# Attention stage of a decoder: block probabilities without zeros, another order on TensorE, doubled parts of z

## The chip, the cores and the metric

The kernel runs on one core of one Trainium2 chip, in one launch. The metric is the device time of one execution in microseconds (us), from runs of the kernel before and the kernel after on the same chip. The engines are TensorE (PE in the profile, with its weight loads in a row of their own, PEld), VectorE (DVE), ScalarE (ACT), GpSimd (POOL) and SyncE (SP), whose queue issues the DMAs.

## What is computed

A two-layer decoder over 32 sequences of 64 tokens with width 256 (2048 tokens, 16 tiles of 128). The change lies in the first of its stages, the self-attention of layer 0: 16 heads of 128, causal, with a layer norm ahead of it.

```
x = x + attention(layernorm(x))                       # the first stage
q = einsum('bpd,hde->bphe', x, W_Q) + b_Q             # k and v alike, with W_K and W_V
scores = einsum('bqhe,bkhe->bhqk', q, k) / sqrt(128)  # 64 x 64 per sequence and head
attn = softmax(where(causal, scores, -100000))
z = einsum('bkhe,bhqk->bqhe', v, attn)
out = einsum('bqhe,hed->bqd', z, W_O) + b_O
```

The stages after it (a cross attention and a feed-forward network, then layer 1) are the same in both kernels.

## The kernel before

**Tiles and units.** A tile holds 128 tokens, that is two sequences of 64. `stage_L0_attention` works in 64 units: 16 heads times 4 groups of 4 tiles (512 tokens). A matmul that needs more precision than fp32r has runs in three products of high and low parts (`PARTS`): the tokens `xnT`, the weights `w_parts` and `wv_parts` and the weighted values `zT` each exist as a high and a low part. Scores, turned probabilities and weighted values are plain fp32 matmuls.

**One unit** goes through these steps:
- TensorE: `project` (queries and keys of 4 tiles, 6 matmuls of 512 columns each), and for the even heads also `values`, which serves two heads at once: 12 matmuls of 256 columns before the queries (tiles 0 and 1) and 12 after the keys (tiles 2 and 3). `scores`: 8 matmuls, one per sequence; the two sequences of a tile write to the two halves of the partitions. `turn`: 4 transposes of the probabilities. `weigh`: values times probabilities, one matmul per tile. `output`: 12 matmuls with W_O.
- ScalarE copies out of PSUM (`v_copy(0)`, `q_copy`, `k_copy`, `v_copy(1)`, `probT_copy`), takes the exponential (`exponent`) and makes the high part of z (`z_high_part`).
- VectorE masks the scores, finds the greatest and subtracts it (`shift`), sums, inverts and multiplies (`normalise`), makes the low part of z (`z_low_part`) and adds the output to the tokens (`add_out`).

**Zeros.** The probabilities of one tile lie in a 128x128 square `prob[:, t, :]` with two 64x64 blocks on its diagonal, one per sequence; the rest was set to zero once (line 674), so that one transpose and one matmul per tile serve both sequences.

**Order of the work.** Each engine has a list of parts with a lag, and `run_steps` goes through it: in step s, part p handles unit s - lag. Within a step an engine takes its parts in the order of the list, strictly one after the other; semaphores hold it where another engine is not ready. Before the change TensorE's list is project (lag 3), turn (4), scores (3), output (5), weigh (4). A round is 8 steps: units 0 to 3 belong to an even head (with values: a **value step**), units 4 to 7 to an odd one (without: a **plain step**).

**Beside it.** In the same lists runs the preparation of two things. First, the weights of a later head: SP loads them (`load`, lines 432 to 449), ScalarE makes the high part (`split_high`, lag 0, at the second unit of each head; for an even head also the value weights, line 615), GpSimd the low part (`split_low`). Second, the dequantisation of the last layer's weights (`Dequantiser`), one of 16 pieces per 4 units: VectorE works in phases 0 to 3 (lines 2466 to 2487) at lag 3, ScalarE in phases 0 (two instructions, lines 2496 and 2498) and 3 (line 2503) at lag 4, GpSimd adds (`gpsimd_sum`, behind `split_low` in its queue) and makes the low part; SP stores the piece.

The load of a head's weights first waits for the outputs of the head two before it, whose buffers it takes; it stands on SP's queue, and ScalarE's splitting waits for the same count and for the load:

```
wait(sp, o_full, (h - 2) * G + G)                      # line 434, SP, before the loads of head h
act.wait_ge(w_in[slot], (rnd + 1) * 48)                # line 610, ScalarE, unit 4 h + 1
wait(act, o_full, u - 5)                               # line 611
```

`prob`, `zT` and `z_ps` are single buffers; each of the eight PSUM banks has one use (`q_ps`, `k_ps`, `v_ps`, `s_ps`, `pT_ps`, `z_ps` and two of `o_ps`).

Of the kernel before, what the change touches and what calls it, by code (L numbers as in the profile page):

```python
# [16 lines left out]
P = 128  # L17
# [257 lines left out]
def split_tokens(core, parts, mv, factor, tag, column_step=1, beside=None, high_beside=None):  # L275
# [7 lines left out]
    with ExitStack() as ctx:  # L283
# [6 lines left out]
        def rows(t):  # L290
            return turned[:, t % 4, 0:D].rearrange("p (c q) -> p c q", c=NC)

        @block.vector
        def _(dve):
            def low(t):
                dve.wait_ge(high_done, t + 1)
                nc.vector.tensor_tensor(parts[:, 1, :, t, :], rows(t), parts[:, 0, :, t, :], ALU.subtract) \
                    .then_inc(low_done, 1)
# [17 lines left out]
        def _(act):  # L316
            for t in range(NT):
                act.wait_ge(turned_done, t + 1)
                nc.scalar.activation(parts[:, 0, :, t, :], rows(t), ACT.Copy).then_inc(high_done, 1)
# [85 lines left out]
def stage_L0_attention(core):  # L405
# [6 lines left out]
    with ExitStack() as octx:  # L412
        oroom = Room(nc, octx, "s1")
        xnT = oroom.sb("xnT", [P, 2, NC, NT, P], F32R)
# [65 lines left out]
        split_tokens(core, xnT, mv, rstd, "s1t", beside=low_weights, high_beside=high_weights)  # L480
        with ExitStack() as ctx:
# [3 lines left out]
            v = room.sb("v", [P, G, TG, 2, E])  # L485
# [5 lines left out]
            prob = room.sb("prob", [P, TG, P])  # L491
            probT = room.sb("probT", [P, TG * P])
            zT = room.sb("zT", [P, 2, TG * P], F32R)
# [3 lines left out]
            s_ps = room.ps("s_ps", [P, 512])  # L497
            pT_ps = room.ps("pT_ps", [P, 512])
            z_ps = room.ps("z_ps", [P, 512])
            o_ps = room.ps("o_ps", [P, 2, 512])  # L500
            (q_full, k_full, v_full, s_full, pT_full, z_full, q_out, k_out, v_out,
             masked, maxed, shifted, exped, summed, inverted, prob_done, pT_out, z_high, z_low, o_out, zeroed) = room.sems(
                "q_full", "k_full", "v_full", "s_full", "pT_full", "z_full",
                "q_out", "k_out", "v_out", "masked", "maxed", "shifted", "exped", "summed", "inverted",
                "prob_done", "pT_out", "z_high", "z_low", "o_out", "zeroed")
# [19 lines left out]
            def _(pe):  # L525
# [3 lines left out]
                def values(u, g, half):  # L529

                    wait(pe, v_out, u + g + half)
                    for n in range(2):
                        t = 2 * half + n
                        for c in range(NC):
                            for px, pw in PARTS:
                                last = nc.tensor.matmul(v_ps[:, n * 2 * E:(n + 1) * 2 * E],  # L536
                                                        xnT[:, px, c, g * TG + t, :], wv_parts[:, pw, c, :, :],
# [4 lines left out]
                def project(u, rnd, k):  # L542
# [7 lines left out]
                    for m, ps, full, out in ((0, q_ps, q_full, q_out), (1, k_ps, k_full, k_out)):  # L550
                        wait(pe, out, u)
                        for c in range(NC):
                            for pw, px in PARTS:
                                last = nc.tensor.matmul(ps[:, :], weights(slot, pw, m, c),  # L554
# [4 lines left out]
                    if slot == 0:  # L559
                        values(u, g, 1)  # L560
# [2101 lines left out]
```

## Time and profile before

| | us |
|---|---|
| three timed runs | 1759.6 to 1762.84, median 1762.19 |
| the profiled execution's own time | 1760.59 |
| its span, first to last instruction | 1758.8 |
| TensorE busy in the span | 1589.2 (90%) |
| VectorE busy | 1088.3 (62%) |
| ScalarE busy | 863.8 (49%) |
| GpSimd busy | 672.6 (38%) |

The profile has one row per instruction or group of instructions: the line of the kernel, the engine, the operation, what it writes and reads, how many (x), how long. PE rows are matmuls, PEld rows the loads of their stationary operand; the two overlap, and the ends of matmuls are modelled, so distances between starts tell more than durations. "128x64" tiles are parts of TensorE's array that work side by side (rows x columns; printed as 128*64). "Idle before" is how long the engine stood before the row, and what released it. "issue" is idle time in which the engine waited for nothing that the profile shows. The first stage's loop lies between about 30 and 562 us of the span.

### The profile page before, as it was taken

How to read it: one execution, taken by the hardware profiler on the slowest of the kernel's cores; microseconds unless marked ns; L12 is line 12 of the kernel's file. 1: busy time of each engine (PE TensorE's matmuls, PEld its weight loads, DVE VectorE, ACT ScalarE, POOL GpSimd, SP SyncE). 2: the span in 40 equal slices, each digit the busy share in tenths (PEclk: the TensorE clock that was granted, in tenths of full speed). 3: DMA queues.
4: the chain of work that ended last, by engine and by line, in shares of the span. 5: the costliest groups of instructions: out<-in, count | busy, mean ns of one | idle time of the engine just before them, and what ended most of it. 6: DMA issues, size and time to landing. Idle time of an engine off the chain costs nothing. (4 is left out here: it accounts for less than half of the span.)

```text
span 1758.8 us, 37012 instructions
## 1 busy us (share of the span) xinstructions
PE 1589.2 (90%) x14664; PEld 1283.0 (73%) x14664; DVE 1088.3 (62%) x1734; ACT 863.8 (49%) x1466; POOL 672.6 (38%) x527
## 2 busy tenths in 40 slices
PE   6999999999997887799999797899997898999998
PEld 4888888888885665687788564566664675888887
DVE  5767777677777888566442468999994564111111
ACT  3545555555453565555422346666672674222222
POOL 0121211211212662531432255999994430233332
PEclk9999999999998998899999799999998897999999
DMA  3011111011112300000102020000000900000000
GB/s 104 16 64 52 43 63 59 33 63 60 39 56 83 104 2 26 8 12 11 40 1 105 23 69 1 1 2 1 2 1 26 358 17 1 1 13 9 4 12 12
DMA packets 72351, 70.26 MB, mean 40 GB/s; under 512 B 24816, under 2 KB 64368, under 8 KB 71840
## 3 DMA queue, kind: packets, MB, share of 16 engines
q1 hardware_dynamic: 72224, 68.46, 12.1%
q8 instruction: 93, 1.52, 0.4%
q14 instruction: 34, 0.28, 0.1%
HBM read 46.03 MB, written 19.27 MB: 37 GB/s over the span
## 5 line engine op out<-in xcount | busy, mean ns | idle before, releaser
L662 POOL TENSOR_TENSOR s_w_parts<-s_w_raw,s_w_parts 128x768 fp32r<-128x768 f32 x15 | 27.8, 1855 | 402.8 <-ACT s_w_parts L612 402.8
L1484 DVE TENSOR_TENSOR s6f_hid<-s6f_act_sb,s6f_u_ps 128x512 f32<-128x512 f32 x64 | 44.0, 688 | 219.5 <-PE s6f_u_ps L1435 219.5
L1507 POOL TENSOR_TENSOR s6f_hid_parts<-s6f_hid,s6f_hid_parts 128x512 fp32r<-128x512 f32 x64 | 82.7, 1293 | 225.9 <-ACT s6f_hid_parts L1473 225.9
L2223 POOL TENSOR_TENSOR s4b_with_q<-s4b_with_q 128x1024 f32<-128x1024 f32 x64 | 150.9, 2381 | 0.4 <-DVE s4b_with_q L2178 0.4
L2178 DVE TENSOR_TENSOR s4b_with_q<-s4b_c_ps,s_q_rows 128x2048 f32<-128x2048 f32 x64 | 146.1, 2284 | 1.2 <-PE s4b_c_ps L2317 1.2
L595 PE MATMUL s_o_ps<-s_w_parts,s_zT 128*128 128x256 f32 x768 | 110.1, 293 | 4.2 <-DVE x_rows L698 4.1
L536 PE MATMUL s_v_ps<-s_wv_parts,s_xnT 128*128 128x256 f32 x768 | 104.8, 286 | 8.2 <-ACT s_v L641 6.8
L1473 ACT ACTIVATE s6f_hid_parts<-s6f_hid 128x512 fp32r<-128x512 f32 x64 | 40.5, 633 | 145.0 <-PE s6f_o_ps L1455 140.8
L536 PEld LDWEIGHTS s_v_ps<-s_wv_parts,s_xnT 128*128 128x128 f32 x768 | 97.2, 191 | 13.8 <-ACT s_v L641 10.0
L1455 PEld LDWEIGHTS s6f_o_ps<-s6w_parts,s6f_hid_parts 128*128 128x128 f32 x768 | 99.1, 188 | 6.6 <-issue 1.0
L595 PEld LDWEIGHTS s_o_ps<-s_w_parts,s_zT 128*128 128x128 f32 x768 | 96.8, 192 | 8.8 <-issue 4.5
L1435 PE MATMUL s6f_g_ps<-s_zT,s6w_parts 128*128 128x512 f32 (+1 forms) x384 | 101.9, 401 | 1.2 <-PEq L283 1.2
L554 PE MATMUL s_q_ps<-s_xnT,s_w_parts 128*128 128x512 f32 x384 | 102.5, 403 | 0.0
L1455 PE MATMUL s6f_o_ps<-s6w_parts,s6f_hid_parts 128*128 128x256 f32 x768 | 100.5, 279 | 0.8 <-POOL s6f_hid_parts L1507 0.8
L1435 PE MATMUL s6f_u_ps<-s_zT,s6w_parts 128*128 128x512 f32 (+1 forms) x384 | 101.1, 399 | 0.0
L625 ACT ACTIVATE s_ex<-s_sc 128x256 f32<-128x256 f32 x64 | 26.7, 418 | 149.1 <-DVE s_sc L690 149.1
L554 PE MATMUL s_k_ps<-s_xnT,s_w_parts 128*128 128x512 f32 x384 | 98.5, 392 | 0.0
L2301 PE MATMUL s4b_turns_ps<-s_theta_parts,s_z_parts 128*128 128x512 f32 x192 | 62.8, 435 | 26.3 <-DVE s4b_frac L2161 24.5
L1435 PEld LDWEIGHTS s6f_u_ps<-s_zT,s6w_parts 128*128 128x128 f32 x384 | 73.0, 190 | 17.7
L554 PEld LDWEIGHTS s_k_ps<-s_xnT,s_w_parts 128*128 128x128 f32 x384 | 72.1, 188 | 15.8
L1507 POOL TENSOR_TENSOR s3f_hid_parts<-s3f_hid,s3f_hid_parts 128x512 fp32r<-128x512 f32 x32 | 42.3, 1320 | 104.9 <-ACT s3f_hid_parts L1473 104.9
L1435 PEld LDWEIGHTS s6f_g_ps<-s_zT,s6w_parts 128*128 128x128 f32 x384 | 68.8, 191 | 13.9 <-issue 1.6
(333 smaller groups left out, 3994.6 us busy)
## 6 DMA issues: line engine op xcount, KB each, us to landing
stored_weights<-s1q_halves SPq DMA_DIRECT2D x16, 768.0 KB, 3.7
s6w_parts<-stored_weights SPq DMA_DIRECT2D x32, 384.0 KB, 7.8
s1q_packed<-in_codes SPq DMA_DIRECT2D x8, 384.0 KB, 4.4
s1q_scale<-in_scale_rows SPq DMA_DIRECT2D x8, 384.0 KB, 4.9
s3p_raw<-in_ffn_pieces SPq DMA_DIRECT2D x8, 384.0 KB, 9.1
early_values<-s_vbd SPq DMA_DIRECT2D x1, 2176.0 KB, 12.3
s_vbd<-early_values SPq DMA_DIRECT2D x4, 544.0 KB, 7.5
x_rows<-in_x SPq DMA_DIRECT2D x4, 512.0 KB, 5.7
```

The costliest lines, as they stand in the source:

```text
L536: last = nc.tensor.matmul(v_ps[:, n * 2 * E:(n + 1) * 2 * E], xnT[:, px, c, g * TG + t, :], wv_parts[:, pw, c, :, :], start=(c == 0 and (p ...
L554: last = nc.tensor.matmul(ps[:, :], weights(slot, pw, m, c), xnT[:, px, c, g * TG:(g + 1) * TG, :], start=(c == 0 and (pw, px) == PARTS[0] ...
L595: last = nc.tensor.matmul(o_ps[:, t // 2, (t % 2) * D:(t % 2 + 1) * D], zT[:, pz, t * P:(t + 1) * P], w_parts[:, k // G, pw, 2, :], start= ...
L662: nc.gpsimd.tensor_tensor(w_parts[:, slot, 1, :, :], w_raw[:, slot, :, :], w_parts[:, slot, 0, :, :], ALU.subtract).then_inc(w_low, 1)
L1435: last = nc.tensor.matmul(ps[:, s, :], wt(pw, c, f), zT[:, pz, c:c + 1, bass.ds(rnd * TG, TG), :] .rearrange("p c t q -> p (c t) q"), star ...
L1455: last = nc.tensor.matmul(o_ps[:, t, 0:D], hid_parts[:, f % 2, ph, t * P:(t + 1) * P], down_w(pw, f), start=(f == 0 and (ph, pw) == PARTS[0]),
L1473: nc.scalar.activation(hid_parts[:, f % 2, 0, :], hid[:, f % 2, :], ACT.Copy).then_inc(high_done, 1)
L1484: nc.vector.tensor_tensor(hid[:, f % 2, :], act_sb[:, f % 2, :], u_ps[:, f % 2, :], ALU.mult) \
L1507: nc.gpsimd.tensor_tensor(hid_parts[:, f % 2, 1, :], hid[:, f % 2, :], hid_parts[:, f % 2, 0, :], ALU.subtract).then_inc(low_done, 1)
L2178: nc.vector.tensor_tensor(with_q[:, half, :, :, :, :, :].rearrange("p (a n) q j s c -> p n a q (j s) c", n=2) [:, n_, :, :, :, :], src.uns ...
L2223: nc.gpsimd.tensor_tensor(with_q[:, half, :, 0, :, n_, :], with_q[:, half, :, 0, :, n_, :], with_q[:, half, :, 1, :, 1 - n_, :], op).then_ ...
L2301: last = nc.tensor.matmul(turns_ps[:, :], z_parts[:, pz, half, bass.ds(i * P, P)], theta_parts[:, pt, half, n_ * 512:(n_ + 1) * 512], star ...
```

## The change

- The tokens `xnT` of a pair of tiles are stored by sequence instead of by tile: first sequence 0 of both tiles, then sequence 1 of both (`pairs=True` in `split_tokens`).
- The probabilities are stored without zeros: `prob[:, k % 2, t, :]` is 128x64 per tile, and it is doubled. One multiplication writes all of it, where two wrote the two blocks. Two tiles side by side make one 128x128 square, so that two transposes serve four tiles, and the copy out of PSUM is 256 columns wide instead of 512.
- The weighting is now 8 matmuls of 64 rows and 64 columns, one per sequence: the rows of tile n of a pair are the partitions 64 n to 64 n + 63 of `v` and `probT`, and the two row halves write to different banks of `z_ps`.
- `z_ps` takes two banks; for that, scores and turned probabilities share one bank (`sp_ps`), with two new waits: the scores wait until the turned probabilities of two units before are copied, and turning waits until the scores of the following unit are masked.
- `zT` is doubled; `z_high_part` waits for the output of one unit earlier.
- TensorE's list becomes queries with the first values (lag 3), turn (5), keys (3), weigh (5), second values (3), output (6), scores (3). ScalarE's list becomes v_copy(0), q_copy, probT_copy (5), k_copy, z_high_part (5), v_copy(1), exponent, split_high, dequantising. VectorE's becomes z_low_part (5), shift, add_out (6), normalise, dequantising. SP's and GpSimd's lists stay as they are.

The diff, cut to its core:

```diff
-        xnT = oroom.sb("xnT", [P, 2, NC, NT, P], F32R)
+        xnT = oroom.sb("xnT", [P, 2, NC, NT // 2, 2, 2, S], F32R)
...
-            prob = room.sb("prob", [P, TG, P])
-            probT = room.sb("probT", [P, TG * P])
-            zT = room.sb("zT", [P, 2, TG * P], F32R)
+            prob = room.sb("prob", [P, 2, TG, S])
+            probT = room.sb("probT", [P, TG * S])
+            zT = room.sb("zT", [P, 2, 2, 2, 2 * P], F32R)
...
-            s_ps = room.ps("s_ps", [P, 512])
-            pT_ps = room.ps("pT_ps", [P, 512])
-            z_ps = room.ps("z_ps", [P, 512])
+            sp_ps = room.ps("sp_ps", [P, 512])
+            s_ps, pT_ps = sp_ps[:, 0:TG * S], sp_ps[:, TG * S:2 * TG * S]
+            z_ps = room.ps("z_ps", [P, 2, 512])
...
                 def scores(u, rnd, k):
                     pe.wait_ge(q_out, u + 1)
                     pe.wait_ge(k_out, u + 1)
                     wait(pe, masked, u)
+                    wait(pe, pT_out, u - 1)
...
                 def turn(u, rnd, k):
                     pe.wait_ge(prob_done, u + 1)
                     wait(pe, pT_out, u)
-                    for t in range(TG):
-                        last = nc.tensor.transpose(pT_ps[:, t * P:(t + 1) * P], prob[:, t, :], core.c("ident"))
+
+                    pe.wait_ge(masked, min(u + 2, U) if isinstance(u, int) else u + 2)
+                    for pair in range(2):
+                        last = nc.tensor.transpose(pT_ps[:, pair * P:(pair + 1) * P],
+                                                   prob[:, k % 2, 2 * pair:2 * pair + 2, :].rearrange("p t s -> p (t s)"),
+                                                   core.c("ident"))
...
                 def weigh(u, rnd, k):
...
-                    for t in range(TG):
-                        last = nc.tensor.matmul(z_ps[:, t * P:(t + 1) * P], v[:, k % G, t, k // G, :],
-                                                probT[:, t * P:(t + 1) * P], start=True, stop=True)
+                    for pair in range(2):
+                        for b in range(2):
+                            for n in range(2):
+                                rows, at = slice(n * S, (n + 1) * S), pair * P + b * S
+                                last = nc.tensor.matmul(z_ps[:, n, at:at + S], v[rows, k % G, pair, b, k // G, :],
+                                                        probT[rows, at:at + S], start=True, stop=True)
...
-                run_steps(pe, U, [(project, 3), (turn, 4), (scores, 3), (output, 5), (weigh, 4)], unroll=8)
+                run_steps(pe, U, [(project_q, 3), (turn, 5), (project_k, 3), (weigh, 5), (second_values, 3), (output, 6),
+                                  (scores, 3)], unroll=8)
...
                 def z_high_part(u, rnd, k):
 
                     act.wait_ge(z_full, u + 1)
-                    wait(act, o_full, u)
-                    nc.scalar.activation(zT[:, 0, :], z_ps[:, :], ACT.Identity, bias=bias[:, k // G, 2:3]) \
+                    wait(act, o_full, u - 1)
+                    nc.scalar.activation(zT[:, k % 2, 0, :, :], z_ps[:, :, 0:2 * P], ACT.Identity, bias=bias[:, k // G, 2:3]) \
                         .then_inc(z_high, 1)
 
-                run_steps(act, U, [(v_copy(0), 3), (q_copy, 3), (k_copy, 3), (v_copy(1), 3), (probT_copy, 4), (exponent, 3),
-                                   (z_high_part, 4), (split_high, 0), (deq.scalar, 4)], unroll=8)
+                run_steps(act, U, [(v_copy(0), 3), (q_copy, 3), (probT_copy, 5), (k_copy, 3), (z_high_part, 5),
+                                   (v_copy(1), 3), (exponent, 3), (split_high, 0), (deq.scalar, 4)], unroll=8)
...
-                nc.vector.memset(prob[:, :, :], 0.0).then_inc(zeroed, 1)
-                dve.wait_ge(zeroed, 1)
-
...
-                    for b in range(2):
-                        rows = slice(b * S, (b + 1) * S)
-                        last = nc.vector.tensor_tensor(prob[rows, :, b * S:(b + 1) * S], ex[rows, :, :],
-                                                       rs[rows, :].unsqueeze(2).to_broadcast([S, TG, S]), ALU.mult)
-                    last.then_inc(prob_done, 1)
-
-                run_steps(dve, U, [(shift, 3), (normalise, 3), (z_low_part, 4), (add_out, 5), (deq.vector, 3)],
+                    wait(dve, pT_full, u - 1)
+                    nc.vector.tensor_tensor(prob[:, k % 2, :, :], ex[:, :, :],
+                                            rs[:, :].unsqueeze(2).to_broadcast([P, TG, S]), ALU.mult) \
+                        .then_inc(prob_done, 1)
+
+                run_steps(dve, U, [(z_low_part, 5), (shift, 3), (add_out, 6), (normalise, 3), (deq.vector, 3)],
                           unroll=8)
```

## Rows read from the trace of the kernel before

**Rows 1.** Windows: stretch, length, busy us (instructions) per engine, granted clock, DMA

```profile
45.00:552.00 507.00, 481.79 (x3949) 429.77 (x3948) 372.56 (x653) 264.47 (x441) 93.79 (x53) 1.00 0.15 49
...
548.00:555.00 7.00, 4.76 (x24) 4.36 (x24) 4.59 (x9) 0.93 (x2) 0.00 (x0) 0.76 0.00 0
```

**Rows 2.** Waits of 45:552: engine, tile, line, releaser; us in total, times, longest

```profile
PE s_s_ps L569 <- issue: 13.0, 31, 0.6
...
PE s_v_ps L536 <- ACT s_v L641: 6.8, 7, 1.2
...
SPq L436 <- PE s_o_ps L595: 234.5, 14, 47.7
```

**Rows 3.** Timeline of a value step: start us, us, engine, line, operation, tiles, count

```profile
304.77 1.48 PEld L536 LDWEIGHTS s_v_ps<-s_wv_parts,s_xnT 128*128 128x128 f32 x12
...
306.18 1.24 PEld L554 LDWEIGHTS s_q_ps<-s_xnT,s_w_parts 128*128 128x128 f32 x6
...
308.83 1.59 PEld L536 LDWEIGHTS s_v_ps<-s_wv_parts,s_xnT 128*128 128x128 f32 x12
...
310.37 0.46 PEld L577 LDWEIGHTS s_pT_ps<-const,s_prob 128*128 128x128 f32 x4
...
311.00 0.55 PEld L569 LDWEIGHTS s_s_ps<-s_kT,s_qT 128*64 128x64 f32 x16 [0.17 <-issue]
...
311.62 1.49 PEld L595 LDWEIGHTS s_o_ps<-s_w_parts,s_zT 128*128 128x128 f32 x12
...
311.73 0.43 DVE L684 TENSOR_TENSOR s_sc<-s_s_ps,const 128x256 f32<-128x256 f32 x1 [3.04 <-PE s_s_ps L569]
...
313.03 0.98 PEld L586 LDWEIGHTS s_z_ps<-s_probT,s_v 128*128 128x128 f32 x8
313.11 0.42 ACT L625 ACTIVATE s_ex<-s_sc 128x256 f32<-128x256 f32 x1 [1.35 <-DVE s_sc L690]
```

**Rows 4.** Timeline of 0.2 us in layer 1's attention, weight loads in 64x128 tiles

```profile
1099.42 0.30 PEld L2340 LDWEIGHTS s4b_y_ps<-s_w_bd,s4b_outT 64*128 64x128 f32 x4 [0.17 <-issue]
```

**Rows 5.** Groups by shape, 45:700: count | busy us, mean ns | idle before

```profile
L679 DVE SCALAR_TENSOR_TENSOR s_zT<-s_z_ps,s_bias,s_zT 128x512 fp32r<-128x512 f32 x64 | 48.1, 752 | 4.7 <-ACT s_zT L650 2.7
...
L890 ACT ACTIVATE s_xT<-s_x_ps 128x256 f32<-128x256 f32 x16 | 6.1, 384 | 31.7 <-PE s_x_ps L915 31.7
```

**Rows 6.** Timeline of a plain step: weighting, the DMA issues behind it, ScalarE's queue

```profile
335.75 0.97 PEld L586 LDWEIGHTS s_z_ps<-s_probT,s_v 128*128 128x128 f32 x8
...
337.90 0.34 SPq L443 DMA_DIRECT2D s_w_raw<-in_L_attn_W_O  x1
...
338.45 0.93 ACT L2498 ACTIVATE s1q_over<-s1q_code,const 128x768 f32<-128x768 int32 x1
338.49 0.93 SPq L448 DMA_DIRECT2D s_wv_raw<-in_L_attn_W_V  x2
...
339.28 0.68 ACT L620 ACTIVATE s_qT<-s_q_ps,s_bias 128x512 f32<-128x512 f32 x1
...
339.85 0.68 ACT L633 ACTIVATE s_kT<-s_k_ps,s_bias 128x512 f32<-128x512 f32 x1
```

**Rows 7.** DMA issues of 45:552: count, KB each, median us to landing

```profile
s_w_raw<-in_L_attn_W_O SPq DMA_DIRECT2D x14, 128.0 KB, 2.4
```

**Rows 8.** Timeline, an even head's weight splitting and what follows on GpSimd and VectorE

```profile
344.45 0.84 ACT L612 ACTIVATE s_w_parts<-s_w_raw 128x768 fp32r<-128x768 f32 x1
...
345.19 0.62 ACT L615 ACTIVATE s_wv_parts<-s_wv_raw 128x512 fp32r<-128x512 f32 x1
345.37 1.85 POOL L662 TENSOR_TENSOR s_w_parts<-s_w_raw,s_w_parts 128x768 fp32r<-128x768 f32 x1 [24.18 <-ACT s_w_parts L612]
...
347.17 1.27 POOL L666 TENSOR_TENSOR s_wv_parts<-s_wv_raw,s_wv_parts 128x512 fp32r<-128x512 f32 x1
...
348.40 1.83 POOL L2509 TENSOR_TENSOR s1q_over<-s1q_over 128x768 f32<-128x768 f32 x1
...
350.27 2.58 DVE L2479 TENSOR_TENSOR s1q_sized<-s1q_over,s1q_code 128x768 f32<-128x768 f32 x1 [3.67 <-POOL s1q_over L2509]
```

## What the change will do, told before it ran

> **What bounds the kernel now.** The change touches the first stage only, so I read the windows view first, over that stage's loop: from 45 to 552 us TensorE is busy 481.8 of 507 us, at a granted clock of 1.00, the higher of its two levels, 2.4 GHz [rows 1]. TensorE sets the pace. The view of waits says what it still loses there: 13.0 us before the scores and 6.8 us before the second value group, seven times [rows 2]. The same view shows the DMA queue's wait for the output matmuls, 234.5 us in 14 times [rows 2]; that wait matters below. Then I read the timeline of one value step (first half of a round, units 0 to 3) [rows 3]. By starts of first loads: values 1.41 us, queries and keys 2.65, second values 1.54, turning 0.63, scores 0.62, output 1.41, weighting eight loads at 0.113 = 0.90; sum 9.16. A plain step (units 4 to 7) has no values: 24 loads less at (1.48-0.19)/11 = 0.117, so 9.16-2.81 = 6.35 of work.
>
> Two details of that timeline carry the rest. Entering and leaving a differently tiled array costs time: the four transposes are 0.107 apart, so of their 0.63 about 0.20 is the way into the scores' 128x64 tiles; eight pairs of score loads at 0.059 make 0.47 of 0.62, so 0.15 is the way out [rows 3]. And VectorE starts masking 0.73 after the scores' first load, the exponential 1.38 after that [rows 3]. I call the start of masking T0; the next step's matmuls begin then too.
>
> **Part by part: TensorE's own work.** Two transposes instead of four: -0.21 per unit. Weighting: eight fp32 matmuls of 128 columns in two passes are 16 loads in eight pairs after the change (two row tiles side by side), eight single ones before. What does a pair of 64x128 loads take? The last layer's heads have that tile: four loads span 0.30 with 0.19 the last, so the second pair starts 0.11 after the first [rows 4]. Eight pairs are then 0.88 to 0.9, what the eight single loads take now. The lower bound is the scores' pair rate, 0.059 [rows 3], worth -0.42; but those loads have 64 columns, not 128, so I take 0.11. New are a way into row tiles and a way out: 0.35 as around the scores, and 0.05 more as the exposed first load is twice as wide: +0.40 (lower bound 0.35). Net +0.19 per unit, 12 us over 64 units; a value step is 9.35, a plain one 6.54. The Trainium skill speaks against the weighting's part too ("TensorE: Matmul & The Clock Gate", LDWEIGHTS): a load's time follows its columns and not its rows, about P/1.2 ns, 107 ns for 128. By that, halving the rows saves nothing; rows 4 agree with 110 ns.
>
> **Removed waits.** Keys are now followed by weighting and output before the scores, so the copy of the keys is covered: -13.0. The value wait of 6.8 has the same cause as a stall that I price anew below, so I take it off and count the new one: -6.8. VectorE saves one of two multiplications, ScalarE half a copy; neither engine ends a wait of its own by work alone, so nothing is counted but the shorter copy below. Doubled buffers only loosen waits. The removed clearing lies beside the first values. One more step of lag lengthens the tail by a few us and the scores' move shortens it as much: within 3 us either way.
>
> **Added: ScalarE's order.** ScalarE takes its queue in order. The exponential of step s now waits for scores that stand at the very end of TensorE's step s, and behind it are this step's weight splitting and dequantising, then the next step's copies of values, queries and turned probabilities. Weighting in the next step waits for that last copy. TensorE is there after queries and keys (2.65 by first loads [rows 3]; I take 2.77, as loads run up to 0.1 further ahead of the wide matmuls), turning 0.21 and a way in of 0.1 (in a value step after 1.40 of values, 12 x 0.117, too): T0+3.08 in a plain step, T0+4.48 in a value step. ScalarE: exponential at 1.38; the next instruction starts 0.10 before the end of one (0.93 long, 0.83 apart; 0.68 long, 0.57 apart [rows 6]), so +0.32; queries +0.57; a copy of 128x256 from PSUM 0.38 [rows 5]; hand-over 0.08 (344.45+0.84 to 345.37 [rows 8]). Ready at 2.73: slack 0.35 in a plain step, about 0.4 in a value step, where the queries come later. Whatever ScalarE has between the exponential and those copies beyond the slack is TensorE's wait, as weighting stands ahead of values, output and scores in its own queue:
> - before a plain step: two dequantising instructions (2 x 0.83 = 1.66), wait 1.3; one of 0.84 (0.75 apart), wait 0.4
> - before a value step: 1.66 leaves 0.4; 0.75 leaves nothing
> These come once a round each: 2.1 x 8 = 17 us.
>
> **Added: the weights' loads, moved past their user.** The load of a head's raw weights waits on SP for the outputs of the head two before. With output at lag 5 this came one step before ScalarE splits those weights; with lag 6 it comes in the same step, 0.73 before T0. Now: the last output load ends where weighting begins (335.75), the loads of W_O and of W_V's second half start at 337.90 and 339.05 (338.49+0.93-0.37) [rows 6] and land 2.4 later [rows 7] (the value pieces are of the same size). So W_O is there 4.6 and W_V 5.7 after the output's end: T0+3.9 and T0+5.0, where ScalarE is free at T0+1.7. In order:
> - even heads (7 times, before a plain step): split to 4.8, value split 5.0 to 5.6; queries' copy at 5.55 instead of 1.72, wait 3.83-0.35 = 3.5. GpSimd then needs 1.80, 1.23 and 1.83 [rows 8]: VectorE's dequantising step runs from 9.75 to 12.25, a subtraction of z (0.75 [rows 5], 0.65 apart), masking at 12.9. The new wait of turning for masking, two steps on: TensorE is there at 6.54+3.5+2.8 = 12.8, masking ends 13.3, wait 0.6; the chain exponential, values, queries, probabilities then ends at 16.1 where weighting could start at 15.2, wait 0.9. Sum 5.0
> - odd heads (7 times; the first was loaded at the start): queries' copy at 5.2 instead of 3.0, wait 1.7; a step later 0.3. Sum 2.0
> Together 7 x 7.0 = 49 us. Bounds: had the weights been there, 7 x 2.8 = 20; each us of later landing adds 14.
>
> **Sum.** +12 -13.0 -6.8 +17 +49 = +58. The profiled execution took 1760.59 (span 1758.8 and 1.8 around it), so 1818.8; the median of the three timed runs is 1.6 above it: **1820 us**.
>
> **Rivals.**
> - *Tiles at the scores' rate.* If the row tiles stream at 0.059 a pair, 64 x 0.42 = 27 us come off: 1793. For it: half the columns stream. Against: rows 4. The Trainium skill promises this case ("TensorEngine Tiling (Array Packing)", Theoretical Speedup): up to twofold where the contraction is at most 64. No weighting in such tiles stands in this trace. Chance 0.10.
> - *The weights are there in time*, because the transfer starts or lands sooner than I place it: 20 for 49, 1791. Against: the queue waits for just these outputs [rows 2]. Chance 0.07.
> - *ScalarE isn't in TensorE's way: faster.* Place: between the exponential and the copy of turned probabilities. If that copy is always there before T0+3.08 and T0+4.48, the 17 and 49 vanish: 1762.2+12-19.8 = 1754, faster than before. It decides at 0.35 us of slack. For it: ScalarE is busy 264 of 507 us [rows 1]. Against: the queue's order, and 3.9 us for a landing. Chance 0.10, and 0.03 more that it holds in most steps only, which ends within 0.2% of before.
> - *The clock falls in the new gaps.* After the idle stretches of the tail the granted clock is 0.76 over 548 to 555 [rows 1], and TensorE was busy only 4.76 of those 7 us. The new gaps of 3.5 us stand between busy stretches. A plain step at the lower of its two levels would cost up to 6.5 us more, none if the clock holds; 3 in each of seven rounds make +21, 1841. Chance 0.10.
> - *The tiles don't run side by side*, so that the change doesn't do what it says: 8 x 0.11 more per unit, 56 us: 1876. Against: the two loads of a pair in rows 4 fit in one load's time. Chance 0.03.
>
> **How the numbers follow.** My own sum has 0.57, between 1800 and 1840 (3 us of tail, a quarter of the 66 us of waits). The two milder cases reach down to 1791, the clock's up to 1841 and, at twice that price half the time, above: range **1788 to 1856**, which leaves out the faster case and the serial tiles. A change within 0.2% (3.5 us, about what a measurement of this kernel can tell) needs the waits to be nearly, but not wholly, gone: same 0.03. Faster 0.10, slower 0.87.
>
> **What would show it.** Right: ScalarE's weight splitting waiting some 2 us for a DMA, 14 times; TensorE waiting before the weighting for the copy of turned probabilities, longest about 3.5; 64x128 loads 0.11 apart in pairs; plain steps near 6.5 only behind a step without dequantising; the first stage some 55 to 60 us longer and the others unchanged. Wrong: splitting that starts behind the exponential at once, weighting that follows the keys without a gap, or pairs 0.06 apart.

## The result and the profile after

The change makes the kernel slower: 1809.51 us median (1804.22 to 1811.9), beside 1762.51 of the kernel before in the same runs; ratio 1.027, 95% interval 1.0253 to 1.0286. The prediction was 1820, range 1788 to 1856. The profiled execution took 1811.9 us, its span is 1810.1.

By the first instruction of the second stage, the first one ends at 611.2 us of the span instead of 563.5: 47.7 of the 51.3 us by which the spans differ lie in it.

The windows view of the first stage's loop, and of three of its rounds, each from the scores of one unit to those eight units on (columns as in [rows 1]; a round of before is 65.0 us):

```profile
45.00:600.00 555.00, 505.38 (x4333) 430.41 (x4333) 338.18 (x586) 247.75 (x443) 93.54 (x54) 0.96 0.14 45
```

```profile
59.26:131.21 71.95, 66.03 (x561) 56.55 (x561) 46.12 (x77) 32.22 (x57) 11.99 (x7) 0.95 0.12 38
...
203.32:274.71 71.39, 64.61 (x561) 55.19 (x560) 42.80 (x75) 32.00 (x57) 11.98 (x8) 0.98 0.15 48
274.71:345.75 71.04, 63.43 (x561) 53.80 (x561) 42.84 (x75) 31.89 (x57) 12.02 (x8) 1.00 0.14 48
```

TensorE was busy 481.8 of 507 us before [rows 1]; now it stands still for 50 of 555, and the granted clock of the loop is 0.96 instead of 1.00. The view of waits over the same stretch says for what (us in total, times, longest):

```profile
PEld s_z_ps L608 <- ACT s_probT L652: 64.8, 47, 3.7
...
PE s_z_ps L608 <- ACT s_probT L652: 47.8, 49, 3.3
...
ACT s_w_parts L635 <- DMA s_w_raw<-in_L_attn_W_O: 22.7, 14, 1.9
...
ACT s_wv_parts L638 <- DMA s_wv_raw<-in_L_attn_W_V: 2.4, 6, 0.7
...
PE s_sp_ps L594 <- DVE s_sc L704: 1.7, 3, 0.6
```

Both waits of [rows 2] that the change was to remove are gone. In their place stands one: the weighting (L608) waits 49 times for ScalarE's copy of the turned probabilities (L652), together 47.8 us, and ScalarE's splitting of the weights (L635) waits 14 times for W_O. One odd head shows the whole chain, in the timeline of TensorE, ScalarE and SP's queue:

```profile
333.68 1.49 PEld L617 LDWEIGHTS s_o_ps<-s_w_parts,s_zT 128*128 128x128 f32 x12
...
335.30 0.55 PEld L584 LDWEIGHTS s_sp_ps<-s_kT,s_qT 128*64 128x64 f32 x16
...
335.91 1.45 PEld L540 LDWEIGHTS s_v_ps<-s_wv_parts,s_xnT 128*128 128x128 f32 x12
...
337.29 1.22 PEld L569 LDWEIGHTS s_q_ps<-s_xnT,s_w_parts 128*128 128x128 f32 x6
337.32 0.35 SPq L448 DMA_DIRECT2D s_w_raw<-in_L_attn_W_O  x1
...
338.88 1.23 PEld L569 LDWEIGHTS s_k_ps<-s_xnT,s_w_parts 128*128 128x128 f32 x6
...
339.48 0.85 ACT L635 ACTIVATE s_w_parts<-s_w_raw 128x768 fp32r<-128x768 f32 x1 [1.66 <-DMA s_w_raw<-in_L_attn_W_O]
340.24 0.58 ACT L664 ACTIVATE s_v<-s_v_ps 128x512 f32<-128x512 f32 x1
340.71 0.68 ACT L643 ACTIVATE s_qT<-s_q_ps,s_bias 128x512 f32<-128x512 f32 x1
341.28 0.38 ACT L652 ACTIVATE s_probT<-s_sp_ps 128x256 f32<-128x256 f32 x1
...
341.72 0.97 PEld L608 LDWEIGHTS s_z_ps<-s_probT,s_v 64*128 64x128 f32 x16 [1.60 <-ACT s_probT L652]
```

W_O starts at 337.32, two microseconds behind the last output, and lands 2.16 later; the splitting has waited 1.66 by then. Copies of values, queries and turned probabilities follow in ScalarE's order, and the weighting starts 1.60 late.

To see where each kernel stands I took, from the rows of the scores' loads, the distance from one unit's first load to the next unit's, in the fourth full round (units 27 to 35), in us. The columns are the steps of one round, from the scores of unit k to those of unit k+1; the second line says what ScalarE has behind the exponential there (deq is dequantising). Steps 7-0 to 2-3 contain values. Every kernel below is here; the runs e1 to e9 are told in the next section. Of the seven full rounds of after, this is the only one with a granted clock of 1.00 from end to end; the other six have 0.95 to 0.98 and take 71.4 to 72.2 us.

```
            3-4   4-5   5-6   6-7    7-0    0-1   1-2   2-3    round
            -     1 deq 2 deq split  -      1 deq 2 deq split
                              even                      odd
before      6.75  6.78  6.90  6.78  10.31   9.16  9.16  9.16   65.0
after       6.78  7.04  7.73  9.43  10.79   9.21  9.59 10.45   71.0
e1          6.48  7.00  7.72  7.33  11.47   9.21  9.60  9.21   68.0
e2          6.73  6.47  6.49 11.02   9.47   9.21  9.21 10.63   69.2
e3          6.48  6.47  6.49  7.33  11.49   9.21  9.21  9.21   65.9
e4          6.47  6.49  6.47  7.23   9.47   9.21  9.21  9.21   63.8
e5          7.62  9.07  6.90  9.56  10.62   9.16  9.16  9.91   72.0
e6          6.95  6.95  6.95  7.71   9.77   9.71  9.71  9.71   67.5
e7          6.47  6.49  6.47  6.49   9.27   9.21  9.21  9.21   62.8
e8          6.47  6.50  7.11  7.23   9.27   9.21  9.21  9.21   64.2
e9          6.47  6.49  6.47  6.49  11.24   9.21  9.21  9.21   64.8
```

In the line of after, beside that of e7, in which these waits are gone, the steps are longer in which ScalarE has something behind the exponential (0-1 alone is not), most of all those with the splitting, and so are the two right behind a splitting (3-4 and 7-0).

### The profile page after: what moved, and what is told of

It reads as the page before. It is cut to its first block and busy times, and to the rows that moved or that the text cites. A ratio compares the mean times of both kernels' runs of the same rounds, so it can differ in the third digit from the quotient of the medians.

```text
span 1810.1 us, 37849 instructions
## 1 busy us (share of the span) xinstructions
PE 1617.8 (89%) x15048; PEld 1287.6 (71%) x15048; DVE 1053.6 (58%) x1669; ACT 846.0 (47%) x1466; POOL 670.4 (37%) x527
## 5 line engine op out<-in xcount | busy, mean ns | idle before, releaser
L617 PE MATMUL s_o_ps<-s_w_parts,s_zT 128*128 128x256 f32 x768 | 116.8, 307 | 1.4 <-DVE x_rows L718 1.4
L608 PEld LDWEIGHTS s_z_ps<-s_probT,s_v 64*128 64x128 f32 x1024 | 63.9, 191 | 74.0 <-ACT s_probT L652 64.8
L608 PE MATMUL s_z_ps<-s_probT,s_v 64*128 64x64 f32 x1024 | 72.7, 282 | 47.9 <-ACT s_probT L652 47.8
L617 PEld LDWEIGHTS s_o_ps<-s_w_parts,s_zT 128*128 128x128 f32 x768 | 105.9, 208 | 4.1 <-issue 1.7
L569 PE MATMUL s_k_ps<-s_xnT,s_w_parts 128*128 128x512 f32 x384 | 104.4, 407 | 0.0
L699 DVE SCALAR_TENSOR_TENSOR s_zT<-s_z_ps,s_bias,s_zT 128x512 fp32r<-128x512 f32 x64 | 47.9, 748 | 64.3 <-ACT s_zT L673 64.3
```

What stands on the lines that cost most here:

```text
L569: last = nc.tensor.matmul(ps[:, :], weights(slot, pw, m, c), xnT[:, px, c, g * 2:g * 2 + 2, :, :, :] .rearrange("p a b t s -> p (a b t s)" ...
L608: last = nc.tensor.matmul(z_ps[:, n, at:at + S], v[rows, k % G, pair, b, k // G, :], probT[rows, at:at + S], start=True, stop=True)
L617: last = nc.tensor.matmul(o_ps[:, t // 2, (t % 2) * D:(t % 2 + 1) * D], zT[:, k % 2, pz, t % 2, t // 2 * P:(t // 2 + 1) * P], w_parts[:, k ...
L699: nc.vector.scalar_tensor_tensor(out=zT[:, k % 2, 1, :, :], in0=z_ps[:, :, 0:2 * P], scalar=bias[:, k // G, 2:3], in1=zT[:, k % 2, 0, :, : ...
```

## The experiments

My theory going in: W_O and W_V land late, and with the dequantising they hold ScalarE's later copies, for which the weighting at the head of TensorE's queue waits. The rivals: the dequantising alone; TensorE's own work in row tiles.

**e1: the raw weights loaded early.** They need only their own raw buffers, free since GpSimd's low part; only the biases need the outputs.

```diff
         def load(sp, h, rnd, slot):
-            wait(sp, o_full, (h - 2) * G + G)
-            src = ins["bias_L0"].rearrange("h e b -> e h b")
-            sp.dma_start(bias[:, slot:slot + 1, :], src[:, bass.ds(h, 1), :]).then_inc(bias_in[slot], 16)
             wait(sp, w_low, h - 1)
...
+            wait(sp, o_full, (h - 2) * G + G)
+            src = ins["bias_L0"].rearrange("h e b -> e h b")
+            sp.dma_start(bias[:, slot:slot + 1, :], src[:, bass.ds(h, 1), :]).then_inc(bias_in[slot], 16)
```

> The kernel after, with SP's loads of the raw weights (W_Q, W_K, W_O, W_V) placed ahead of the wait for the outputs of the head two before; only the load of the biases, which needs that wait, stays behind it. The order on every engine but SP is untouched. My theory (the landing of W_O and W_V holds ScalarE, and ScalarE's late copies hold TensorE before the weighting): the two ScalarE waits for a DMA (22.7 and 2.4 us) vanish, the wait before the weighting falls from 46.9 to some 22 to 26 us, and the time from 1809.5 to 1783 to 1788 (my priced difference was 29 us; the measured waits are three quarters of the priced ones). Rival A (the dequantising instructions alone make the wait): within 3 us of 1809.5. Rival B (TensorE's own work in row tiles is dearer than before, and the waits only fill its slack): within 3 us of 1809.5.

Measured: 1780.9 us, 28.6 less than after, and 2 below my range. No ScalarE wait for a DMA is left. The weighting's wait over the loop, and one that has grown:

```profile
PE s_z_ps L608 <- ACT s_probT L652: 28.4, 40, 1.6
...
PE s_sp_ps L594 <- DVE s_sc L704: 9.6, 8, 2.2
```

The priced difference was 29 (49 against 20). That the two agree so well is partly luck: in the fourth round, where both kernels have a clock of 1.00, e1 is 3.0 us shorter, 21 us in seven rounds; in after's other rounds the clock is lower, and part of the 28.6 is its return to 1.00 (in all full rounds of e1 but the first). Step 2-3 falls from 10.45 to 9.21 and step 6-7 from 9.43 to 7.33; the steps with dequantising stay at 7.00, 7.72 and 9.60. Step 7-0 rises from 10.79 to 11.47, as turning (L594) now waits for masking there; e3 shows why. Both rivals expected no change; as the whole story they fall.

**e2: dequantising ahead of the exponential**, in the idle time in which ScalarE waits for the scores. The loads stay late.

```diff
-  (v_copy(1), 3), (exponent, 3), (split_high, 0), (deq.scalar, 4)]
+  (v_copy(1), 3), (deq.scalar, 4), (exponent, 3), (split_high, 0)]
```

> The kernel after, with the dequantising instructions ahead of the exponential in ScalarE's list; the weights' splitting stays behind it and SP's loads stay late. My theory: only the waits behind a dequantising step go (priced 17 us, 2.1 a round; with the measured ones three quarters of it): 1792 to 1797, and ScalarE still waits some 22 us for W_O. Rival A (the dequantising alone makes the wait before the weighting): that wait goes from 46.9 to under 5 and the time to about 1763. Rival B (TensorE's own work): within 3 us of 1809.5.

Measured: 1795.1, 14.4 less than after, and ScalarE still waits 25.0 us for W_O, 14 times. Steps 4-5, 5-6 and 1-2 are now 6.47, 6.49 and 9.21: that part of the wait is the dequantising, and no more than that. (The 11.02 in 6-7 holds a fall of the clock, which is granted at 0.96 over 45 to 550 us, as in after.)

**e3: both.**

> The kernel after with both edits, early loads of the raw weights and dequantising ahead of the exponential; the splitting of the weights still stands behind the exponential. My theory: the two savings add up, some 34 to 46 us, to 1764 to 1776; what is left of the wait before the weighting is the splitting itself (0.84 us for an odd head, about 1.4 to 1.6 for an even one, once per head), 10 to 15 us in all, so the kernel does not get below the kernel before by more than its uncertainty. Rival A (one cause): the time equals that of the better of the two single edits within 3 us. Rival B (TensorE's own work): 1806 to 1812.

Measured: 1764.6, 45.0 less than after, where the two savings make 43.0 if added. Two causes, each with a price of its own. Left over are 6-7 (7.33) and 7-0 (11.49), the steps at and behind the splitting for an even head. In 7-0 TensorE waits first for VectorE, not for ScalarE:

```profile
351.66 1.84 POOL L2534 TENSOR_TENSOR s1q_halves<-s1q_full,s1q_halves 128x768 fp32r<-128x768 f32 x1
351.73 2.58 DVE L2498 TENSOR_TENSOR s1q_sized<-s1q_over,s1q_code 128x768 f32<-128x768 f32 x1 [2.96 <-POOL s1q_over L2528]
...
354.89 0.41 DVE L704 TENSOR_TENSOR s_sc<-s_sp_ps,const 128x256 f32<-128x256 f32 x1
...
355.45 0.41 PE L594 MATMUL s_sp_ps<-const,s_prob 128*128 128x128 f32 x2 [1.09 <-DVE s_sc L704]
```

GpSimd's sum, queued behind its work on the split weights, is late; VectorE's dequantising step waits for it and takes 2.58 us beside GpSimd's next instruction; masking stands behind that, and turning waits 1.1 us for masking; the weighting then waits another 0.8. It is the chain that the prediction gave for an even head, at 0.6 and 0.9.

**e4: the splitting ahead of the exponential too**, which only early loads allow.

```diff
-  (v_copy(1), 3), (deq.scalar, 4), (exponent, 3), (split_high, 0)]
+  (v_copy(1), 3), (split_high, 0), (deq.scalar, 4), (exponent, 3)]
```

> The kernel after with early loads and with both the splitting of the weights and the dequantising ahead of the exponential in ScalarE's list, where ScalarE stands idle for the scores anyway. My theory: nothing of ScalarE's is left between the exponential and the copies of queries and turned probabilities, the wait before the weighting falls below 5 us, the granted clock of the loop returns to 1.00, and the time is 1740 to 1757: what was removed (13.0 and 6.8 us) then shows, less some 3 us of own work. Rival A (ScalarE's order is not the cause): no lower than the run with both edits and the splitting behind the exponential. Rival B (TensorE's own work in row tiles is dear by 10 us or more): the waits go, but the time stays above 1757 to 1762.

Measured: 1750.7, ratio to before 0.9936 (0.9919 to 0.9952): 0.6% faster than the kernel before. The granted clock over 45 to 543 us is 1.00 again. What the splitting's move saves is step 7-0, which falls from 11.49 to 9.47, so it comes off the chain over GpSimd and VectorE; 6-7 only falls from 7.33 to 7.23. The weighting's wait did not quite fall below 5: 9.3 us are left, 17 times, up to 1.1, all but one in steps 6-7 and 7-0. There ScalarE is not to blame. GpSimd, VectorE and what follows, in the timeline of e4 (rows of two answers, by engine):

```profile
336.31 1.85 POOL L685 TENSOR_TENSOR s_w_parts<-s_w_raw,s_w_parts 128x768 fp32r<-128x768 f32 x1 [23.03 <-ACT s_w_parts L635]
338.11 1.48 POOL L689 TENSOR_TENSOR s_wv_parts<-s_wv_raw,s_wv_parts 128x512 fp32r<-128x512 f32 x1
```

```profile
336.41 0.42 DVE L708 TENSOR_REDUCE s_mx<-s_sc 128x4 f32<-128x256 f32 x1
336.87 1.58 DVE L710 TENSOR_TENSOR s_sc<-s_sc,s_mx 128x256 f32<-128x256 f32 x1
338.37 1.21 DVE L718 TENSOR_TENSOR x_rows<-x_rows,s_o_ps 128x1024 f32<-128x1024 f32 x1
```

```profile
338.48 0.42 ACT L648 ACTIVATE s_ex<-s_sc 128x256 f32<-128x256 f32 x1 [1.72 <-DVE s_sc L710]
...
339.37 0.37 ACT L652 ACTIVATE s_probT<-s_sp_ps 128x256 f32<-128x256 f32 x1
...
339.80 0.97 PEld L608 LDWEIGHTS s_z_ps<-s_probT,s_v 64*128 64x128 f32 x16 [1.11 <-ACT s_probT L652]
```

VectorE's subtraction (L710) takes 1.58 us instead of 0.42 and ends 0.3 behind GpSimd's first instruction, and the exponential and the copies come that much later. That made e7.

**e5: the late loads alone, on the kernel before.**

```diff
-            wait(sp, o_full, (h - 2) * G + G)
+            wait(sp, o_full, (h - 2) * G + G + (0 if isinstance(h, int) and h < 2 else 1))
```

> The kernel before, with one thing of the change alone: the loads of a head's weights wait for one more output, so that they come in the same step in which ScalarE splits them (as they do after the change), while TensorE, ScalarE and VectorE keep the order of before. My theory (a transfer that starts at the end of an output and lands 4 to 5 us later holds ScalarE, and what is queued behind it holds TensorE): ScalarE waits 14 times for W_O, each about 1.5 to 2.5 us, and the time rises from 1761 by 15 to 35 us; here the copies of queries, keys and values are what comes late. Rival A (the late transfer hurts only together with the new order, in which the weighting stands ahead of three other groups): within 4 us of 1761. Rival B (late loads do not hold ScalarE in any order): no ScalarE wait for a DMA, within 4 us.

Measured: 1802.9, ratio 1.0237 (1.022 to 1.0254), 43 us more than before; more than I expected. The waits over its loop:

```profile
DVE s1q_sized L2479 <- POOL s1q_over L2509: 80.2, 15, 6.6
...
ACT s_w_parts L612 <- DMA s_w_raw<-in_L_attn_W_O: 35.8, 14, 2.9
...
PE s_s_ps L569 <- ACT s_qT L620: 23.0, 8, 3.5
```

ScalarE waits 14 times, 2.6 us each at 35.8/14, and one step of lag in a load costs an otherwise unchanged kernel nearly what the whole change cost. My 15 to 35 counted ScalarE's wait alone; the table shows the excess over before not only in the steps of the splitting (+2.78 and +0.75) but also in 3-4 (+0.87) and 4-5 (+2.29). In two rounds in which the clock is 1.00 through step 4-5 that step takes 7.53 and 7.52, so about 1.5 of the 2.29 is a fall of the clock (0.81 granted in that step). The rest fits VectorE's longer wait for GpSimd's sum (80.2 us against 43.6 in before), which no run here takes apart. Rivals A and B fall.

**e6: the weighting's row halves one after the other** (on e4).

```diff
-  for pair in range(2):
-      for b in range(2):
-          for n in range(2):
+  for n in range(2):
+      for pair in range(2):
+          for b in range(2):
```

> The best kernel so far (1750.7: early loads, splitting and dequantising ahead of the exponential) with the weighting's eight matmuls in another order: first the four of the upper row half, then the four of the lower one, so that neighbouring loads go to the same row half. My theory (the two loads of a pair run side by side only because they alternate between the halves, 0.11 us a pair as measured): 16 loads at 0.11 instead of eight pairs, 0.8 to 0.9 us more in each of 64 units, +45 to +56 us, 1796 to 1807. Rival A (a load of 64 rows takes half the time wherever it goes): within 3 us of 1750.7. Rival B (the matmuls and not the loads set the pace, and they overlap whatever the order): within 3 us, or up to 10 more.

Measured: 1786.5, 35.8 more than e4. One weighting in e6, read in three views that end when 5, 12 and all 16 loads have started, and below one in after (start, span of the group, engine):

```profile
308.25 0.63 PEld L608 LDWEIGHTS s_z_ps<-s_probT,s_v 64*128 64x128 f32 x5 [0.36 <-issue]
308.25 1.02 PEld L608 LDWEIGHTS s_z_ps<-s_probT,s_v 64*128 64x128 f32 x12 [0.36 <-issue]
308.25 1.47 PEld L608 LDWEIGHTS s_z_ps<-s_probT,s_v 64*128 64x128 f32 x16 [0.36 <-issue]
309.78 1.46 PEld L540 LDWEIGHTS s_v_ps<-s_wv_parts,s_xnT 128*128 128x128 f32 x12
```

```profile
321.67 0.97 PEld L608 LDWEIGHTS s_z_ps<-s_probT,s_v 64*128 64x128 f32 x16 [0.36 <-issue]
322.71 1.45 PEld L540 LDWEIGHTS s_v_ps<-s_wv_parts,s_xnT 128*128 128x128 f32 x12
324.08 1.49 PEld L617 LDWEIGHTS s_o_ps<-s_w_parts,s_zT 128*128 128x128 f32 x12
325.70 0.55 PEld L584 LDWEIGHTS s_sp_ps<-s_kT,s_qT 128*64 128x64 f32 x16
```

So the two halves do run side by side, and the order of issue sets how much of the time they do. With a load 0.19 long, the alternating pairs of after come every (0.97-0.19)/7 = 0.111 us. In e6 the first five loads are (0.63-0.19)/4 = 0.110 apart, the next seven (1.02-0.63)/7 = 0.056, the last four (1.47-1.02)/4 = 0.11. That fits two series of eight, each 0.11 apart, the second begun when the first has three loads to go. So loads to one half do come every 0.11 us, as I had expected, but the halves still overlap for a part of the group: it is 0.50 longer and not 0.8 to 0.9, and 64 x 0.50 = 32 of the 36 us. The Trainium skill's rule ("TensorE: Matmul & The Clock Gate", LDWEIGHTS), that a load's time follows its columns alone (by it 107 ns for 128), fits both: 111 ns for the pairs and 110 ns for loads of 64 rows to one half.

**e7: GpSimd's list turned round, and kept clear of VectorE's subtraction** (on e4). The dequantiser's low part and sum, ready one and two steps earlier, no longer queue behind the weights' low part; each of the three waits until the subtraction of its step is done.

```diff
                 def split_low(h, rnd, slot):
...
+                    pool.wait_ge(shifted, h * G - 1)
                     pool.wait_ge(w_high, h + 1)
...
+                def behind_shift(count):
+                    pool.wait_ge(shifted, min(count, U) if isinstance(count, int) else count)
+                def low(j, rnd, slot):
+                    behind_shift(j * G + G + 1)
+                    deq.gpsimd_low(j, slot)
+                def total(j, rnd, slot):
+                    behind_shift(j * G + 2)
+                    deq.gpsimd_sum(j)
-                run_steps(pool, H, [(split_low, 0), (lambda j, rnd, slot: deq.gpsimd_sum(j), 1),
-                                    (lambda j, rnd, slot: deq.gpsimd_low(j, slot), 2)])
+                run_steps(pool, H, [(low, 2), (total, 1), (split_low, 0)])
```

> The best kernel so far (1750.7) with another list on GpSimd: the dequantiser's low part and sum, whose inputs are there one and two steps earlier, ahead of the weights' low part, and each of the three behind VectorE's subtraction of its step. What is left in 1750.7 is 9.3 us of waiting before the weighting, 17 times up to 1.1 us, in the steps where VectorE's subtraction took 1.58 us beside a GpSimd instruction (0.42 elsewhere) and where VectorE's dequantising step stood ahead of masking because it waited for GpSimd's sum. My theory (these two hold VectorE, the exponential comes late, and the copy of turned probabilities behind it): the wait before the weighting falls below 3 us, VectorE's wait for GpSimd's sum from some 70 us to under 10, and the time to 1741 to 1746. Rival A (the rest is ScalarE's own queue, the splitting of 0.84 and 0.61 us): within 2 us of 1750.7. Rival B (GpSimd's instructions now meet other VectorE instructions that matter as much): 1749 to 1756.

Measured: 1744.4, ratio to before 0.9905 (0.9888 to 0.9922), the best of all. TensorE's waits and the windows row of its loop:

```profile
PE s_z_ps L608 <- ACT s_probT L652: 2.9, 3, 1.6
PE s_sp_ps L594 <- DVE s_sc L715: 0.6, 1, 0.6
```

```profile
45.00:533.00 488.00, 484.28 (x4329) 414.43 (x4328) 331.09 (x585) 253.90 (x440) 95.60 (x54) 1.00 0.15 50
```

TensorE is busy 484.3 of 488 us. VectorE is not free of GpSimd there: 43 of the 64 multiplications for the probabilities begin beside it and take up to 1.27 us instead of 0.42, but no wait of TensorE ends with them. The loop is at TensorE's own work, and what the change was worth without its waits can be read off: 62.8 a round instead of 65.0.

**e8 and e9: parts of e7's edit**, e8 the list without the waits, e9 only split_low's wait, on the list as it was. The other two waits were not tried on that list.

> The kernel of 1750.7 us with GpSimd's list turned round alone (low part of the dequantiser, its sum, then the weights' low part), without the wait for VectorE's subtraction that the kernel of 1744.4 us also had. What it tells apart: which of that kernel's two edits brought the 6.3 us. If VectorE's subtraction, held by a GpSimd instruction beside it (1.58 to 2 us instead of 0.42), is what makes the exponential late, the subtraction now meets the sum too, in the step after two dequantising instructions, and some 15 or more of the 64 stay long: 1746 to 1752. If only VectorE's wait for the sum mattered, all of the gain is here: 1743 to 1746.

> The kernel of 1750.7 us with only the other edit: GpSimd's low part of the weights starts behind VectorE's subtraction of the same step, the list is as in the change. The subtraction is then never long (0.42 us in all 64), and the 0.76 us that a plain step per round had beyond 6.48 go (7 times, some 5 us). But the sum, behind it in GpSimd's queue, ends about 0.6 to 0.9 us later, and with it VectorE's dequantising step ahead of the masking of the first value step. If masking is bound by that: the value step takes back 0.6 to 1.4 us each time, 1747 to 1756. If only the subtraction mattered, all of the gain is here: 1743 to 1746.

Measured: 1755.5 and 1757.3, both above e4's 1750.7. Neither brings anything alone. In e8 45 of the 64 subtractions are long (0.46 us or more; 16 in e4, none in e7), and step 5-6 rises to 7.11, as GpSimd's sum now meets the subtraction there. In e9 only one is long and 6-7 is 6.49, but the sum comes later, VectorE's dequantising step takes 2.58 us in 14 of 16 cases beside GpSimd's next instruction (6 of 16 in e4, none in e8), and 7-0 rises from 9.47 to 11.24. Each removes one collision and makes the other worse. My ranges lay on both sides of e4 and were too low, e8's by 3.5 and e9's by 1.3.

## Why the prediction was right, and where its sizes were off

**TensorE's own work: +12 predicted, about +6 measured.** A value step without waits is 9.21 (predicted 9.35), a plain one 6.48 (predicted 6.54): 32 x 0.05 + 32 x 0.13 = 5.8. The price of a pair, 0.11 from [rows 4], was right to the hundredth, and the rival with 0.059 fell. In e7 the way into row tiles is seen as keys taking 1.59 instead of 1.37, the way out as weighting taking 1.04 instead of 0.90: 0.36, I had 0.40. The rows are, of e7 (from keys to second values) and of before (keys, which end at 308.83 in [rows 3]):

```profile
304.86 1.24 PEld L569 LDWEIGHTS s_k_ps<-s_xnT,s_w_parts 128*128 128x128 f32 x6
306.45 0.97 PEld L608 LDWEIGHTS s_z_ps<-s_probT,s_v 64*128 64x128 f32 x16 [0.36 <-issue]
307.49 1.45 PEld L540 LDWEIGHTS s_v_ps<-s_wv_parts,s_xnT 128*128 128x128 f32 x12
```

```profile
307.46 1.33 PEld L554 LDWEIGHTS s_k_ps<-s_xnT,s_w_parts 128*128 128x128 f32 x6
```

The rest is that the groups of values and queries are 0.03 to 0.04 shorter each than in [rows 3]; why, no run here tells.

**Removed waits: -19.8 predicted, about -22 measured.** Neither is in the trace of after. In the table, before's steps exceed its own work (9.16 and 6.35) by 3.0 a round, 22 us in all.

**ScalarE's order: +17 predicted, 14.4 by e2.** 5-6 was to be 6.54+1.3 = 7.84 and is 7.73; 4-5 6.94, is 7.04; 1-2 9.75, is 9.59.

**The late loads and the splitting: +49 predicted; 28.6 for the landing (e1) and 13.8 for the splitting (e3 to e4), 42.4.** The mechanism was as told, 14 times. Of the 28.6 some 21 are the waits at an equal clock (e1, above), and nearly all of the 13.8 lies in 7-0, in the chain over GpSimd and VectorE. The size was off in the landing: I put W_O at T0+3.9; at the odd head above T0 is 335.30+0.73 = 336.03 and the splitting starts at T0+3.45, as the landing took 2.16 instead of 2.4 and the scores start a little later behind the output. ScalarE's wait is 1.6 (22.7/14), not 2.2. Step 6-7 was to be 10.04, 2-3 11.05, and they are 9.43 and 10.45 in the fourth round, without a fall of the clock; 7-0 was to be 10.85 and is 10.79 there. In the other six rounds 6-7 takes 9.74 to 11.65 and 7-0 9.47 to 10.87, so the close hit of 7-0 belongs to one round; the two together were to be 20.89, are 20.22 there and 20.36 to 21.63 in the others.

Undoing ScalarE's waits one after the other makes 1809.5-1750.7 = 58.8 (e4), the return of the clock included, where 17 and 49 were 66: 7.2 too much. The other 3.3 of the 10.5 by which 1820 was too high lie between e4 and the 1754 that the sum gives without these waits: own work is 6 lower and the removed waits are 2 higher, and against that stands what still holds e4, 6.3 by e7. That is GpSimd's hold on VectorE, of which I had 1.5 per even head inside the 49, and which before has as well (14 of its 16 dequantising steps are held). No run gives before e7's list on GpSimd, so what it would gain there is not known. The sign that the first stage would be 55 to 60 us longer came out too high in the same way: 47.7.

**The rivals.** "ScalarE isn't in TensorE's way" gave 1754; about this time came out when ScalarE was moved out of the way (e4, 1750.7), so the term that decided the sign was the right one. How near the two are is partly luck, as own work was priced too high and GpSimd's hold is still in e4. "The clock falls in the gaps" came in part: 0.96 over the loop. The three rounds shown have 0.95, 0.98 and 1.00 and take 72.0, 71.4 and 71.0; all seven together are 5.2 us longer than seven of the fourth, and not 21. In e1, with gaps of up to 1.6 us instead of 3.3, step 5-6 was 7.72 in six of seven rounds, where it is 7.72 to 8.55 in after.

**The other stages** were to stay unchanged. From the second stage's start to the end the span of after is 3.6 us longer; in the experiments, whose code there is the same, this stretch takes 1194.5 to 1199.8 us (before: 1195.3). It varies from one execution to another by about as much, and I count it to nothing.

## What to carry to other kernels

When an order is rewritten, follow what each moved step issues on other queues: a transfer that waits for a moved step moves with it, and here one step of lag in a load cost 43 us in a kernel that was otherwise unchanged. On an engine that works strictly in order, put side work where the engine would wait anyway (ahead of the exponential, not behind it); the same instructions then cost nothing. A change that loses may be a good one with a misplaced neighbour: with loads, side work and GpSimd moved, this one is 1.0% faster than before; how much of that the kernel before would gain from GpSimd's move alone was not tried.

## What the runs showed of the hardware

**VectorE stands still beside GpSimd.** VectorE's subtraction and its multiplication for the probabilities, each with two inputs in SBUF, take 0.42 us alone. In e4 16 of the 64 subtractions and 15 of the 64 multiplications are long, up to 1.99 and 2.07 us: these are the ones that begin while a GpSimd instruction runs, and no other does. The reduction ahead of the subtraction (L708, at 336.41, one input) began beside GpSimd too and took 0.42, and so did the addition of the output behind it (L718, at 338.37, one of its two inputs in PSUM), which took its usual 1.21, as in all of the 15 times that it began there in e4. [rows 8] had it too: VectorE's dequantising step of 2.58 us began while GpSimd worked; where it begins beside none, in e8, it takes 0.95. I had taken 2.58 as that instruction's own time. The Trainium skill states this as an exclusive lock on a shared port pair ("SBUF — State Buffer", SBUF: two separate sides), for VectorE instructions with two SBUF inputs, held for the whole instruction; the trace agrees.

**Loads of 64 rows to one row half come 0.11 us apart, no faster than loads of 128 rows (0.113, [rows 3]); loads to the other half run beside them** (e6). Sixteen loads that alternate between the halves span 0.97 us, eight to one half and then eight to the other 1.47: here the nesting of three loops is worth 36 us.
